# AdaLN block on one core: mask in the attention matrix's place, modulation chunks loaded without waits, batch 0 multiplied by feature blocks

## What is computed

```python
mod = (silu(c) @ wmod).reshape(8, 6, 1, -1)      # wmod is 1024 x 6144
sa, ca, ga, sb, cb, gb = (mod[:, i] for i in range(6))
ga = (2 * (ga >= 0) - 1) * maximum(abs(ga), 0.25)      # gb likewise
h = layernorm(x) * (1 + ca) + sa
attn = einsum('ds,td->st', w1, w2) * sparse_mask       # 1024 x 1024, a band around the diagonal
x = x + ga * gelu(einsum('bds,st->bdt', h, attn) + b2)
h = layernorm(x) * (1 + cb) + sb
H = (h @ U1) @ V1 + b1                                 # rank 256, 2 x 2752 columns
x = x + gb * (((silu(gate) * up) @ U2) @ V2 + b2f)     # gate, up: the halves of H
```

## Time and profile before

| | us |
|---|---|
| median of 3 runs (1196.84 to 1201.61) | 1197.95 |
| the profiled execution | 1196.55 |
| its span, first to last instruction | 1194.7 |
| PE busy | 1143.3 (96%) |
| DVE busy | 587.0 (49%) |
| ACT busy | 491.4 (41%) |
| POOL busy | 390.5 (33%) |
| PE busy between 0 and 50 us | 28.9 |
| PE busy between 160 and 200 us | 40.0 |

### The profile page before, as it was taken

One profiled execution on the slowest core, in us unless ns is written; L12 is line 12 of the kernel. 1 busy time (PEld: TensorE's weight loads), 2 busy tenths in 40 slices (PEclk: granted clock), 3 DMA queues, 4 the chain that ended last, 5 costly groups with the idle time before them and its releaser, 6 DMA issues.

```text
span 1194.7 us, 15376 instructions
## 1 busy us (share of the span) xinstructions
PE 1143.3 (96%) x5882; PEld 943.0 (79%) x5882; DVE 587.0 (49%) x937; ACT 491.4 (41%) x787; POOL 390.5 (33%) x339
## 2 busy tenths in 40 slices
PE   5588999999999999999999999999999999999998
PEld 5357898887778788888888888888888888888886
DVE  1557687786665334434444344443543434344343
ACT  0037577676777543224224323323322432332241
POOL 1007899891112657313031130211303113021110
PEclk9899999999999999999999999999999999999999
DMA  9984998857553642421040150122113015013001
GB/s 358 360 311 149 339 343 302 310 190 271 212 211 129 199 143 79 163 85 71 28 149 3 69 176 1 71 90 87 71 50 127 23 48 176 1 71 122 20 1 70
DMA packets 57197, 169.61 MB, mean 142 GB/s; under 512 B 6176, under 2 KB 10784, under 8 KB 55072
## 3 DMA queue, kind: packets, MB, share of 16 engines
q1 hardware_dynamic: 57120, 168.57, 39.4%
HBM read 126.51 MB, written 42.04 MB: 141 GB/s over the span
## 4 chain that ended last, share of the span: by engine, by line
PE 84%; DMA 4%; DVE 4%; ACT 3%; issue 2%; SPq 1%; POOL 1%; DVEq 0%; ACTq 0%
PE bank L537 23%; PE bank L538 23%; PE bank L539 23%; PE bank L702 6%; PE bank L597 4%; PE bank L576 2%; DMA mask_a<-in_mask 2%; ACT nrm L957 2%; PE bank L688 1%; DMA pt_dram<-pt_st 1%; DVE h_lo L1316 1%; DMA wm_sb<-in_wmod 1%; DVE bn L1183 1%; PE bank L877 1%; SPq L377 1%
## 5 line engine op out<-in xcount | busy, mean ns | idle before, releaser
L1121 ACT ACTIVATE act<-bank,b_sb 128x512 f32<-128x512 f32 (+1 forms) x176 | 121.3, 690 | 497.3 <-PE bank L539 481.4
L1448 DVE SCALAR_TENSOR_TENSOR act<-bank,b_sb,act 128x512 f32<-128x512 f32 (+1 forms) x176 | 131.9, 750 | 376.2 <-PE bank L539 352.8
L537 PE MATMUL bank<-pt,v_hi 128*128 128x512 f32 x688 | 268.8, 391 | 1.3 <-DVE act L1448 1.3
L538 PE MATMUL bank<-pt,v_hi 128*128 128x512 f32 x688 | 267.7, 389 | 0.0
L539 PE MATMUL bank<-pt,v_lo 128*128 128x512 f32 x688 | 267.7, 389 | 0.0
L1599 POOL TENSOR_TENSOR x2t<-gbb_bc,x2t 128x512 f32<-128x512 f32 x64 | 85.4, 1357 | 250.8 <-DMA x2t<-x_dram 250.8
L1458 DVE TENSOR_TENSOR act_lo<-act,act_hi 128x512 fp32r<-128x512 f32 (+1 forms) x176 | 160.5, 912 | 0.9
L537 PEld LDWEIGHTS bank<-pt,v_hi 128*128 128x128 f32 x688 | 129.1, 188 | 31.7 <-DVE act L1448 4.3
L539 PEld LDWEIGHTS bank<-pt,v_lo 128*128 128x128 f32 x688 | 129.2, 188 | 27.1
L538 PEld LDWEIGHTS bank<-pt,v_hi 128*128 128x128 f32 x688 | 129.2, 188 | 26.1
L537 PE MATMUL bank<-act_hi,u_hi 128*128 128x512 f32 x336 | 130.9, 390 | 0.7 <-DVE act_lo L1458 0.6
(11 more groups left out here) (134 smaller groups left out, 1670.0 us busy)
## 6 DMA issues: line engine op xcount, KB each, us to landing
wm_sb<-in_wmod SPq DMA_DIRECT2D x9, 2048.0 KB, 10.3
xs<-in_x SPq DMA_DIRECT2D x32, 512.0 KB, 5.6
x_dram<-xs SPq DMA_DIRECT2D x32, 512.0 KB, 5.1
xs<-x_dram SPq DMA_DIRECT2D x32, 512.0 KB, 5.5
x2t<-x_dram SPq DMA_DIRECT2D x32, 512.0 KB, 4.1
out<-x2t SPq DMA_DIRECT2D x32, 512.0 KB, 4.9
pt_dram<-pt_st SPq DMA_DIRECT2D x8, 1024.0 KB, 7.5
pt<-pt_dram SPq DMA_DIRECT2D x8, 1024.0 KB, 5.7
```

The source lines that it names most:

```text
L537: nc.tensor.matmul(acc, s_hi, m_hi, start=start, stop=False)
L538: nc.tensor.matmul(acc, s_hi, m_lo, start=False, stop=False)
L1121: nc.scalar.activation(act[0:w, j % 2, :], bank[0:w, j % 2, :], ACT.Silu, bias=b1_sb[0:w, i, 0:1]).then_inc(silu_done, 1)
L1448: nc.vector.scalar_tensor_tensor(act[0:w, j % 2, :], up, b1_sb[0:w, i, 1:2], act[0:w, j % 2, :], ALU.add, ALU.mult).then_inc(act_done, 1)
```

## The change

- **Mask.** The mask lies as `mask_sb` in the place of `attn_hi`, which is written over it block by block. `mask_a` and `mask_b` are gone. Its halves are loaded behind pairs 3 and 5 of `w1` and `w2t` instead of behind pair 7.
- **Chunks.** Chunk 0 goes to `wm_first`, behind `w2t_sb`; chunks 1 and 2 to `wm_sb` and `xs2`. Chunk 2 no longer waits; chunk 3 waits for product 1 instead of product 0. The token tiles of batch 1 wait for `dense_past` as well.
- **Norms.** `nrm` is free, so batch 0's norms stand ahead of `attn_hi` in ACT's code.
- **Masked product.** Blocks run from 0 to 7, and DVE takes the rest of block s-1 behind the mask of block s.
- **PE.** `mod_product(0)` stands ahead of the read of `dense_flag`. In `first_batch` outputs 0 to 3 are multiplied together, one feature block after the other (`first_parts`); products 4 and 5, their turns and `first_gates` stand between and behind outputs 4 to 7, and the transposes of batch 1 behind all of it. `beta_product(0)` is cut in two, and the shift is rounded in two halves.
- **DVE and ACT.** The rows follow; all statistics of batch 1 stand behind `mod_place(5)`.
- **Norm halves, second part.** In the U1 part, norms 1 and 3 of the second half move up.

```diff
-        (masked,), _ = tiles_from(LOW + nbytes([P, FB, D]), ("masked", [P, FB, D]))
+        (mask_sb, masked), _ = tiles_from(LOW, ("mask_sb", [P, FB, D]), ("masked", [P, FB, D]))
...
-        (w2t_sb, mask_b), _ = tiles_from(RING_AT, ("w2t_sb", [P, FB, D]), ("mask_b", [P, FB // 2, D]))
+        (w2t_sb, wm_first), _ = tiles_from(RING_AT, ("w2t_sb", [P, FB, D]), ("wm_first", [P, FB, HALF]))
...
-        WM_PLACE = [0, 1, 2, 0, 2] + [0] * (NCHUNK - 5)
-        lent = {1: nrm, 2: xs2}
+        WM_PLACE = [1, 0, 2, 0, 2] + [0] * (NCHUNK - 5)
...
                 sp.dma_start(w2t_sb[:, k, :], w2t[rows, :]).then_inc(w_in[k], 16)
-            for half, tile in enumerate((mask_a, mask_b)):
...
+                if k == 3:
+                    mask_load(0)
+                elif k == 5:
+                    mask_load(1)
             wm_load(0)
             wm_load(1)
-            sp.wait_ge(dense_past, 1)
             wm_load(2)
-            sp.wait_ge(mod_mm, 1)
+            sp.wait_ge(mod_mm, 2)
             wm_load(3)
...
             wm_load(5)
             sp.wait_ge(attn_mm, FB)
+            sp.wait_ge(dense_past, 1)
...
+            pe.wait_ge(consts_made, 1)
+            pe.wait_ge(c_ready, 1)
+            mod_product(0)
             pe.wait_ge(flag_known, 1)
             dense = nc.tensor.value_load(dense_flag[0:1, 0:1].bitcast(I32))
...
-            pe.wait_ge(masked_ready, 2)
-            mod_product(0)
-            mod_turn(0)
-            mod_product(1)
-            mod_turn(1)
-            pe.wait_ge(masked_ready, FB)
+            def first_parts(at):
+                for u in range(TT):
+                    y_near(0, u, at, at + 1)
 
             def first_batch(whole):
+                pe.wait_ge(masked_ready, FB)
                 turn(0, 0)
+                mod_turn(0)
                 turn(0, 1)
+                turn(0, 2)
+                first_parts(0)
+                turn(0, 3)
+                mod_product(1)
+                first_parts(1)
+                mod_turn(1)
+                first_parts(2)
+                turn(0, 4)
+                turn(0, 5)
+                first_parts(3)
                 mod_product(2)
...
+                turn(0, 6)
+                turn(0, 7)
+                mod_turn(2)
+                first_parts(4)
+                beta_first_half()
                 mod_product(3)
...
                 mod_turn(3)
-                turn(0, 7)
+                beta_product(0, whole)
+                beta_product(1, whole)
+                for u in range(TT):
+                    y_end(0, u, whole)
                 mod_product(4)
-                y_near(0, 2)
+                y(0, 4, whole)
                 mod_turn(4)
                 mod_product(5)
-                beta_product(0, whole)
+                y(0, 5, whole)
                 mod_turn(5)
...
+                y(0, 6, whole)
                 pe.wait_ge(mod_placed, 6)
-                pe.wait_ge(beta_lo_ready, 1)
                 gate_turn(6, ga_turned)
...
+                y(0, 7, whole)
                 first_gates()
...
+                for k in range(4):
+                    turn(1, k)
```

ACT's and DVE's code after it, and the U1 part's norms on ACT:

```diff
+            for c in range(2):
+                for n in range(TT):
+                    norm(0, c, n)
+            for n, s in enumerate(range(FB)):
...
-                    for k in range(3):
+                    for k in range(2):
                         hi(t + 1, k)
-                        norm(t + 1, 1, k)
-                    norm(t + 1, 1, 3)
+                        norm(t + 1, 1, 2 * k)
+                        norm(t + 1, 1, 2 * k + 1)
+                    hi(t + 1, 2)
                     hi(t + 1, 3)
...
+            for s in range(FB):
+                dve.wait_ge(attn_mm, s + 1)
                 mask_product(s, s, *band_cols(s), masked_ready)
+                if s > 0:
+                    band_rest(s - 1)
+            band_rest(FB - 1)
...
+            for k in range(4, FB):
+                lo(0, k)
             mod_copy(2)
-            for k in range(2, 6):
-                lo(0, k)
+            mod_place(2)
+            shift_lo(0, 0)
             mod_copy(3)
...
             mod_copy(5)
-            stats(1, 1)
             mod_place(5)
-            beta_lo(0)
-            stats(1, 2)
-            stats(1, 3)
+            for n in range(TT):
+                stats(1, n)
+            aggregate(1)
             dve.wait_ge(ga_turned, 1)
```

201 lines of the change are left out of this document (86 added, 115 removed).

## The result

| | before | after |
|---|---|---|
| median of the runs on one chip | 1197.39 us (1196.48 to 1201.61, 4 runs) | 1211.7 us (1210.07 to 1212.22, 4 runs) |
| span of the profiled execution, granted clock | 1194.7 us, 0.994 | 1210.4 us, 0.981 |

The ratio is 1.011, with a 95% interval of 1.0084 to 1.0136: 14.3 us more. The forecast was 6.5 us more, 1204.5, and a range up to 1210; the time lies above it. The intervals of the ratios are 3 to 7 us wide, so two changed kernels that differ by 2 us or less are not told apart by their times.

A forecast was written before the change was run, and what follows sets the result against it. Bound: when PE can start batch 1 and go on with batch 2, by its own rows or a chain beside them. Batch 1's norms +6.05, end +6.5: 1196.55 becomes 1203.05, median 1.4 above, 1204.5; range 1199.5 to 1210.

The forecast's parts named there:

- The product: Weight product: ends at 46.7, 5.4 later than before, with a stall of 3.2 before pair 6's pass.
- Rival 3: More lost: slower product up to +1.7, branch's fetch up to +3, batch 1 +1; 1206 to 1211; chance 0.25.
- The branch: PE's jump over the dense-mask code, behind product 0: 4.62 us (bounds 3.35 and 4.62), first transpose at 55.0.
- From the first transpose to turn 5: PE in batch 0: 31.8 us of work plus 7.5 of waits, turn 5 at 94.3, 6.4 later than before.
- Behind turn 5: DVE takes batch 1's eight statistics before the gate rows: rows at 101.7, batch 1's norms at 103.5, +6.05.
- Behind the norms of batch 1: Batch 1 onward: lower clock costs 1.5, a later PE wait can take up 1.12; end at +6.5.
- The norm halves of the second part: Norms 1 and 3 of the second half move ahead of h_hi 1 and 2: bounds 0 and -5.5, taken as 0.
- A gain of 8.4 ends as idle time: The 8.4 us gained up to the first transpose end as PE's idle time before batch 1's first output.
- the first: PE's own rows decide, so batch 0's end counts: 5 us faster, 1193; chance 0.08.
- The second: Same chain but shorter: jump 3.35, clock not down, turn 2's wait shorter; +2 to +5, 1200 to 1203; chance 0.22.
- fourth: PE's jump target lies in loaded code, so the jump costs 0.08, 4.5 off; +2, 1200; chance 0.03.

The follow-up runs named there:

- h_late_chunks: Changed kernel with modulation chunks 1 and 2 loaded only behind the first transpose, so no large load runs during PE's branch; 1211.28 us.
- e_masks_last: Changed kernel with both mask halves loaded behind the last weight pair, as before the change; 1213.13 us.
- e_warm: Changed kernel with 52 unused matmuls filling PE's idle time around the gates and between batch 1's transposes; 1211.21 us.
- h_nojump: Changed kernel with PE's dense paths left out, so PE neither reads the flag nor branches; 1204.31 us.
- i_blocks: e_old_batch with near parts of outputs 0 to 3 by feature blocks and products 1 to 3 later; products 4 and 5 keep their old places; 1205.18 us.
- j_blocks: e_old_batch with near parts of outputs 0 to 3 by feature blocks, every modulation product and transpose at its old place; 1197.06 us.
- e_stats: Changed kernel with batch 1's rows loaded earlier and its statistics taken between batch 0's low halves instead of behind turn 5; 1211.3 us.
- f_gates: e_stats with modulation products 4 and 5 back to back and the gates ahead of output 6; 1206.19 us.
- m_old: e_old_batch with PE's dense products moved to the head of the second dense branch, so PE doesn't branch ahead of batch 0; 1189.68 us.
- e_old_batch: Kernel before with the first half of the change alone (loads, masks, early norms, product 0 ahead of the branch), batch 0's order old; 1197.18 us.

## Why the prediction was wrong in size

By its own steps:

- **The product**: forecast to end at 46.7, it ended at 49.0. The forecast stall (3.2) was there (3.90), but the work beside it ran at 1.2 GHz from 38.0 to 44.8. With 5.52 us of matmuls in that stretch, the lower level costs about half, 2.8; the passes ahead were a little quicker than forecast. Rival 3 had "up to 1.7" for this.
- **The branch**: 6.23, outside both bounds (3.35 and 4.62). The upper bound had been taken as one with "its load on the queues", but two chunks were in flight now, where before it was one. That the flag's load ran beside product 0 gave the 1.6 back: from product 0 to the first transpose it took 7.1, as forecast. First transpose at 57.59 instead of 55.0, which is product 0's lateness (50.45 instead of 47.9). Rival 3 had this mechanism and up to 3 us for it; 2.8 were measured by h_late_chunks.
- **From the first transpose to turn 5**: forecast 31.8 of work and 7.5 of waits, 39.3. It took 44.86, of which 5.6 were waits (1.26, 2.38, 0.83 and 1.09 in PE's timeline; the wait for DVE's copy of product 2 was forecast at 2.6). So the work took 39.3 instead of 31.8. **This is the step that failed**, by 7.5: the work was priced at the durations of full clock, with 0.6 for the clock in one place. 13.3 us of matmuls ran at 1.2 GHz (6.44 from 57.6 on, 6.90 from 78.8 on), which adds about half, 6.7. The other 0.8 is work that the sum of 31.8 undercounted. The kernel before had its lower level in the branch's idle time and on 3.1 us of work at 63.4. Together: 2.6 for the first transpose, 7.5 for the work, 1.9 less waiting make the 8.2 by which turn 5 missed 94.3. That it is the clock shows in five kernels with the same matmuls on PE in this stretch, whose clock fell for different lengths (busy time summed over stretches of 0.5 us, mixed ones in proportion):

| kernel | PE busy, first transpose to turn 5 | of it at 1.2 GHz | busy less half of that |
|---|---|---|---|
| after | 39.3 | 13.3 | 32.7 |
| h_late_chunks | 39.1 | 12.9 | 32.7 |
| e_masks_last | 37.6 | 9.6 | 32.8 |
| e_warm | 37.5 | 9.6 | 32.7 |
| h_nojump | 36.3 | 6.5 | 33.0 |

- **Behind turn 5**: right in kind and size. 6.8 us to the gate rows, 9.6 to the norms of batch 1 (102.45 to 112.05), forecast 9.2. Turn 5 was forecast 6.4 later than before and was 14.6 later; the norms were forecast 6.05 later and were 14.6 later.
- **Behind the norms of batch 1**: forecast 1.5 lost to the clock and 1.1 taken up by later waits, 0.45 more in all. Measured: 2.9 more up to batch 2 (14.6 to 17.5), and 1.8 taken up at the beginning of the last part, where PE waited 0.7 us for DVE instead of 1.3 and 0.6; 1.1 more in all (those waits are 1.2 of the 1.8). By e_warm the lower clock is 1.2 of the 2.9 (from the norms at 108.24 to batch 2 it took 41.7 there, 42.95 in the change).
- **The norm halves of the second part**: nothing, as forecast. PE's waits for norms there sum to 5.5 in 7 times, the longest 0.8, in both kernels.
- **"A gain of 8.4 ends as idle time"**: the gain was gone, as forecast, but only a part as idle time. The first transpose was 5.8 ahead mostly because product 1 had moved behind it; with the first half alone it was 1.4 ahead. The forecast took that product for work that may be late. i_blocks against j_blocks shows that it isn't where products 4 and 5 follow at their old places: 8 us. And with the eight statistics out of the way (e_stats) most of the loss stays.

The rivals: the first (PE's own rows decide, faster) fell, as batch 1's norms started far later than 99. The second and fourth asked for a branch of 3.35 or 0.08. The third came nearest (1206 to 1211, and 1211.7 was measured). It had the longer branch in the right size and the slower clock in the weight product too small, and like the forecast it had nothing for the clock between the first transpose and turn 5.

By differences the kernels stand in this row: first half alone -1.7; near parts by blocks with products 1 to 3 behind them, i_blocks, 6.6; f_gates 7.6; e_stats 12.4; the change 14.3. Two of the steps are clear of the intervals: 8.3 to i_blocks, and 4.8 from f_gates to e_stats, where the gates go behind outputs 6 and 7. The 1.9 of the statistics is not, nor the 1.0 from i_blocks to f_gates, between which several things differ (the places of products 4 and 5 and of the transposes, the early statistics, the bias rows and the shift in halves, the norm halves). The steps are differences between whole kernels, and not causes that add up in the changed one: it waits for no chunk. The clock is no further term but sits in them: j_blocks had 1.00 from 70 to 100 us, i_blocks 0.64 in 80 to 90.

What stays open: how much of the 8.3 is the chunk's late load and how much the clock that falls in the waits for it. The two come together in i_blocks, and no run held one fixed. Nor did a run hold the clock up between 57 and 86 in the changed kernel, so what that alone would give at the end isn't measured. e_warm's turn 5 lay 3.1 before that of the change with the same program up to there (1.3 from the start, 1.8 from the clock), so a single profile of these stretches is good to about 3 us.

## What to carry to other kernels

Price the work behind every idle stretch at both clock levels, and let the difference widen the range: here it was 6.6 us by turn 5. A load that may start only when its place has been read can make the reader urgent, however little its result is wanted: before you move such an instruction behind others, follow the loads that it frees to the last one (8 us in i_blocks, nothing in the change, where they had landed in time). And look for a long branch in front of the first busy stretch: moving the rarely used code behind the common path gave 5.6 us in the old kernel and 7.7 with the first half of the change (m_old against e_old_batch), more than any of the reordering gave.
